# Six local attention layers on one Trainium2 core: scores ahead of the output product, softmax shift ahead of the residual addition

## The reference

```
for i in range(DEPTH):                       # DEPTH = 6
    x = attn_layer(shift_tokens(x), ...) + x
    x = ffn_layer(shift_tokens(x), ...) + x

q, k, v = split(x @ Wqkv); q = rope(l2norm(q)); k = rope(l2norm(k))
attn = softmax(mask(q k^T * 8))              # each window sees itself and the one before
out  = (attn v) @ Wo

xn = layernorm(x); a, gate = split(xn @ W1 + b1)
ffn = (a * gelu(gate)) @ W2 + b2
```

## Time and profile before

| | us |
|---|---|
| median of 3 runs | 3092.83 (3081.48 to 3099.36) |
| the profiled execution, its own time | 3103.04 |
| its span | 3101.3 |
| PE busy | 2707.9 (87%) |
| POOL busy | 1833.4 (59%) |
| DVE busy | 1738.0 (56%) |
| ACT busy | 1476.6 (48%) |

### The profile page before, as it was taken

The page is one execution under the profiler, slowest core; times in us unless marked ns, Lnnn a source line. Parts: engine busy times, 40 slices in busy tenths (PEclk is TensorE's granted clock), DMA queues, the critical chain, the costliest instruction groups (busy, mean ns, idle before and its releaser), DMA issues. The chain is left out here.

```text
span 3101.3 us, 91235 instructions
## 1 busy us (share of the span) xinstructions
PE 2707.9 (87%) x37375; PEld 1824.3 (59%) x37375; DVE 1738.0 (56%) x3395; ACT 1476.6 (48%) x2703; POOL 1833.4 (59%) x3112
## 2 busy tenths in 40 slices
PE   4859999965989999989999999999999958999977
PEld 1228888852666666666666666666666635455445
DVE  5832222214767776677767777777777635334324
ACT  3722232212656666566666566656665622233233
POOL 0045666405988888888888887888888711121111
PEclk9967898756999999999999999999999987577668
DMA  1001111102111212122212212121111100000000
GB/s 31 0 22 34 44 38 35 30 17 110 52 42 50 60 52 71 50 57 60 59 48 63 67 52 57 52 78 43 42 49 45 43 11 13 1 1 1 1 12 14
DMA packets 113143, 124.58 MB, mean 40 GB/s; under 512 B 40782, under 2 KB 71262, under 8 KB 111966
## 3 DMA queue, kind: packets, MB, share of 16 engines
q1 hardware_dynamic: 111808, 117.52, 13.8%
q10 hardware_dynamic: 926, 1.27, 0.1%
HBM read 35.89 MB, written 8.91 MB: 14 GB/s over the span
## 5 line engine op out<-in xcount | busy, mean ns | idle before, releaser
L1719 POOL TENSOR_TENSOR l_rot_a<-l_rot_a,l_rot_b 128x512 f32<-128x512 f32 x384 | 483.9, 1275 | 109.8 <-DVE l_rot_b L1579 109.3
L1207 PE MATMUL l_A<-l_wts,l_H 128*128 128x512 f32 x768 | 416.1, 626 | 25.5 <-ACT l_H L1520 21.5
L1573 DVE TENSOR_TENSOR l_rot_a<-l_A,l_tab 128x512 f32<-128x512 f32 x384 | 264.9, 690 | 288.5 <-ACT l_sq L1439 276.2
L1728 POOL TENSOR_TENSOR l_qk<-l_rot_a,l_rn 128x512 f32<-128x512 f32 x384 | 388.7, 1044 | 21.2 <-POOLq L1766 20.9
L1439 ACT ACTIVATE l_sq<-l_A 128x512 f32<-128x512 f32 x384 | 231.0, 601 | 131.9 <-PE l_A L1207 128.3
L1445 ACT ACTIVATE l_pT<-l_T 128x512 f32<-128x512 f32 x192 | 108.8, 595 | 374.0 <-PE l_T L1253 373.7
L1579 DVE TENSOR_TENSOR l_rot_b<-l_A,l_tab 128x512 f32<-128x512 f32 x384 | 261.4, 681 | 0.0
L1583 DVE TENSOR_REDUCE l_ss<-l_sq 128x8 f32<-128x512 f32 x384 | 259.5, 676 | 0.0
L2048 ACT ACTIVATE a_pT<-a_t 128x384 f32<-128x384 f32 (+1 forms) x256 | 111.1, 463 | 261.4 <-PE a_t L1946 261.3
L1308 PE MATMUL l_T<-ident,l_qk 128*128 128x128 f32 x1536 | 210.3, 279 | 19.6 <-POOL l_qk L1728 14.4
L1308 PEld LDWEIGHTS l_T<-ident,l_qk 128*128 128x128 f32 x1536 | 174.9, 142 | 84.1 <-issue 58.0
(11 more groups left out here) (340 smaller groups left out, 5948.0 us busy)
## 6 DMA issues: line engine op xcount, KB each, us to landing
l_vw<-l_vn SPq DMA_DIRECT2D x384, 128.0 KB
l_vw<-l_vn SPq DMA_DIRECT2D x360, 64.0 KB
l_wts<-in_l_wts SPq DMA_DIRECT2D x18, 650.0 KB, 4.9
c_lower_out<-c_amt SPq DMA_DIRECT2D x16, 384.0 KB, 2.5
c_inv<-c_first_in SPq DMA_DIRECT2D x16, 384.0 KB, 3.4
l_tab<-in_l_tables SPq DMA_DIRECT2D x6, 1024.0 KB, 5.1
l_wts<-in_l_wts SPq DMA_DIRECT2D x6, 635.5 KB, 5.3
result<-x SPq DMA_DIRECT2D x4, 256.0 KB, 2.3
```

The lines of the kernel that those rows point to most:

```text
L1207: pe.matmul(A[j % 2][:], cols(m), w_of(m)[:, C_QKV + 512 * j:C_QKV + 512 * j + 512], start=True, stop=True).then_inc(pq_done, 1)
L1573: dve.tensor_tensor(rot_a[p][:, j, :].rearrange("p (a d) -> p a d", d=DH), src.rearrange("p (a d) -> p a d", d=DH), table[:, a, t:t + 1, : ...
L1719: pool.tensor_tensor(rot_a[m % 2][:, j, :], rot_a[m % 2][:, j, :], rot_b[:, j, :], ALU.add).then_inc(rot_rdy, 1)
L1728: pool.tensor_tensor(qk[:, j, :].rearrange("p (a d) -> p a d", d=DH), rot_a[p][:, j, :].rearrange("p (a d) -> p a d", d=DH), rn[p][:, 8 * ...
```

## The change

In PE's loop `scores(n)` is moved ahead of `output(n-2)`. In DVE's loop `soft_shift(n)` is moved ahead of `add_back(n-2)`. No instruction, wait or buffer is added or taken away; ACT, POOL and the transfers keep their order.

```
@@ -1384,10 +1384,10 @@
                     masks(n)
                 if group_at(n, 4) is not None:
                     narrow(group_at(n, 4))
+                if has(n):
+                    scores(n, range(HP))
                 if has(n - 2):
                     output(n - 2)
-                if has(n):
-                    scores(n, range(HP))
                 if group_at(n, 2) is not None:
                     turn_norm(n, group_at(n, 2))
                 if has(n - 1):
@@ -1693,10 +1693,10 @@
                     rope(n + 2, 1)
                 if group_at(n, 4) is not None:
                     feed_back(group_at(n, 4))
+                if has(n):
+                    soft_shift(n)
                 if has(n - 2):
                     add_back(n - 2)
-                if has(n):
-                    soft_shift(n)
                 if has(n + 2):
                     rope(n + 2, 2)
                 if has(n):
```

## The result

| | us |
|---|---|
| before, median of 4 runs | 3096.1 (3081.48 to 3102.11) |
| with the change, median of 4 runs | 3251.2 (3242.33 to 3260.2) |
| ratio | 1.0508, 95% interval 1.0458 to 1.0559 |
| profiled execution, its own time | 3242.33 (before 3103.04) |
| its span | 3240.3 |

The forecast was 3286, with a range of 3235 to 3345. The direction and the range hold; the size, 193 us forecast for a median of 3093, was 155.

A forecast was written before the change was run, and what follows sets the result against it. PE was taken to bound the local layers. Slot costs of 7.25 us a period times 23.5 gave 170 us, plus 23 for the clock: 193 on 3103 gives 3296, less 10 against the median, 3286 us; range 3235 to 3345.

The forecast's parts named there:

- What bounds the kernel: Local layers: PE has 0.3, 0.0 and 0.5 us to spare in kinds 0, 1 and 2; 3.6 in kind 3.
- The scores' move brings nothing by itself: PE's loop: reordering scores and output gains nothing; the wait on ACT's copies it could relieve is 0.7 us in all.
- Kind 0: Slots like 48: the first half of the probabilities' transposes waits for DVE's shift and addition, costing 1.6 us.
- Kind 1: Slots like 49: DVE is held by `feed_back`, then shifts and adds before those transposes, costing 1.35 us.
- Kind 2: Slots like 50: PE already waits for the addition, so the whole shift ahead of it costs 2.5 us.
- The clock term: Slots of kind 2: lower clock after the longer wait in three of four, 1.3 us each, 23 us in all.
- Kind 3: Slots like 51: the shift adds 2.5 us, the wait at `turn_norm` absorbs 0.7, so the cost is 1.8 us.
- rival (a): POOL does not slip in kind 2, so `turn_norm` absorbs its delay and kind 3 costs nothing more: 3222 us; chance 0.06.
- The number of periods: Local layers: 94 slots have both tile n and tile n-2, taken as 23.5 four-tile periods paying the cost.
- Rival (b): The clock falls after every new wait, in kinds 0 and 1 too: up to 3446 us; chance 0.08.
- (c): Faster: an earlier softmax shift shortens the wait at `turn_norm`; half of its 50.5 us gives 3068 us; chance 0.03.
- (d): No measurable change: other PE waits hide the new one, though those in kinds 0 to 2 total 16.1 us; chance 0.03.

The follow-up runs named there:

- the two single-kind runs: The change made only in slots of kind 2, or only of kind 3, on the kernel before: 3137.0 us (+1.3%) and 3150.5 us (+2.1%).

## Why the prediction was right, and what was mis-sized

**What bounds the kernel: right.** PE has no slack in kinds 0 and 1, and a wait put there is paid in full: half 0 comes 1.45 and 1.15 us later in them, and the slots grow by 1.59 and 1.12. (POOL had 3.5 us to spare in slot 48, not the 1 to 3 of the prediction; nothing rests on it.)

**The scores' move brings nothing by itself: right**, shown by the run with PE's move alone, +0.6% and no gain.

**Kind 0, 1.6 forecast: 1.59, to the hundredth by luck.** Half 0 starts at 5.66 us, forecast 5.8, so 1.45 later than before. Most slots of kind 0 went from 16.58 to 18.07, 1.49 more; the rest of the mean comes from a few slots of 18.7 with an issue wait in them.

**Kind 1, 1.35 forecast: 1.12.** The sample misled me. Slot 49 belongs to a group whose `feed_back` has three instructions, one of them for the edge column; in every second group it has two and frees DVE about 0.25 us sooner. In the changed kernel half 0 starts 8.05 us into slot 49 and 7.79 into slot 53. The term was read from the dearer of the two.

**Kind 2, 2.5 and 0.75 x 1.3 for the clock, 3.5 in all: 2.85.** Half 0 comes 2.38 later on average (7.29 against 4.91 us into the slot), near the 2.5. The clock term came out near its size by a different way. The granted clock does fall in slots of kind 2, in 17 of the 22 from slot 4 to 91 (three in four was taken; before, in none); these 17 take 18.53 us and the other five 17.40, so it costs 1.1 a time, 0.87 a period where 0.98 was forecast. But the stretches are 3.4 us long, half the stretch of kind 3 on which I had priced them, and the 1.3 was meant as the share that POOL passes on. What the forecast left out in this kind is that some comes back behind half 0: in the five slots with the clock up PE goes from half 0 to the next masks in 10.10 us against 10.52 before, most of it idle time that is gone (0.22 instead of 0.56). The forecast had such hidden waits only at the lower end of its range. A stretch at the lower level, in slot 46:

```profile
1664.20:1667.60 3.40, 3.22 (x132) 2.41 (x132) 2.27 (x4) 1.98 (x4) 2.65 (x3) 0.51 0.02 5
```

**Kind 3, 1.8 forecast: 1.98.** In slot 50 POOL's `probs` slipped by 1.74 where 1.8 was worked out, and `turn_norm` waits 1.70 in slot 51 where 1.9 was. On average over slots 5 to 88 `turn_norm` starts 0.72 sooner in its slot (0.7 worked out), but its wait falls further, from 2.33 to 1.24, since PE comes to it later; that is why the sum is 27.3 where about 35 was forecast. Half 0 comes 1.67 later, and 0.3 more is lost behind it, where the lower clock now holds for 6.2 us of the slot instead of 5.5 (taken as no change). This step, on which rival (a) hung, is the one that the two single-kind runs test directly.

**The number of periods was the other mis-sized term.** Per period the change costs 7.5 us (80.8 - 73.3), not 8.2. And I multiplied by 23.5. From the masks of slot 4 to those of slot 92, 22 periods, the profiled executions differ by 162.0 us (1776.3 and 1614.3); the first four slots take 61.6 us in both, so the additions of slots 2 and 3 cost nothing there, and the last three slots add 3.9. What hides the first ones was not tried. That gives 166 us for the stretch. The rest of the program, which the change doesn't touch, took 27 us less in this execution (11.3 ahead of slot 0, 15.6 behind slot 95), which is how 139 comes out between the two profiled executions. That is chance: over the ten profiled kernels here the time ahead of slot 0 goes from 736.5 to 763.1 us and that behind slot 95 from 602.3 to 617.9, and no edit touches them. It also means that the 166 of the stretch and the 155 between the medians can't be told apart. The 27 us between the 193 forecast and these 166 are 0.7 a period too much, 16 us, nearly all of it from kind 2, and 11 us for counting 23.5 periods where some 22 have the cost.

**Rival (b), the clock after every new wait, did not come, and its mechanism is real.** In the changed kernel from slot 4 on no stretch at the lower level begins in kinds 0 or 1, where the waits are 0.7 to 1.2 us, as slot 54 had suggested. In the kernel with DVE's move alone the waits there are 2.5 us, and 34 such stretches begin in the 44 slots of kinds 0 and 1. The rule of the Trainium skill ("TensorE: Matmul & The Clock Gate", section "A second HAM failure mode: psum-queue depth-cycling"), that brief idling between groups of matmuls swings the clock, agrees with that kernel (20.60 us for slot 48 with the clock down, 19.30 for slot 44 with it up) and with kind 2 of the change, where waits of 2.3 to 3.0 us were followed by a fall in 17 of 22 slots. It does not agree with kinds 0 and 1 of the change, whose shorter waits leave PE at 2.4 GHz (PEclk 1.00 in slots 48 and 49). In these runs it takes more than that there is a wait: in kinds 0 and 1 no fall followed those of up to 1.2 us, and one followed those of 2.5 us in most slots, not in all.

**Rivals (c) and (d)**: POOL's wait for the reciprocal in kind 2 grew from nothing to 0.73 in slot 50, so an earlier shift shortened nothing; and the issue waits that the new wait could hide fell only from 16.1 to 11.6 us. The waits of half 0 for the addition sum to 201.9 us where some 230 was forecast: 1.2, 0.9, 2.7 and 4.2 by kind for 1.5, 1.2, 3.0 and 4.2.

## What to carry to other kernels

When two steps of a software pipeline share a buffer, the step that frees it belongs in its engine's queue at the moment when its input is ready, not behind work that is long and whose own consumer is not waiting; here 2.5 us of softmax ahead of a 0.6 us addition, with the product that it adds moved back as well, cost 7.5 us per four tiles, and moving the addition the other way won 2.1. Before starting a chain sooner, follow it to the step that ends it: the exponentials stood behind a square that stood behind the very transposes that the move delayed. And where slots alternate, take a term from every variant of the slot, and count how many periods really have it.

## What the runs showed of the hardware that I had not expected

A wait of PE can cost more than it lasts. The waits of 0.7 to 1.2 us in kinds 0 and 1 of the change cost about themselves. With DVE's move alone all slots of kind 0 have the same wait of 2.49 us; where the clock stayed up a slot mostly took 19.30 us, and where it fell to the lower level behind the wait, in 13 of 22, about 20.6. What decides between the two was not found. Lower stretches in the local layers are mostly 3.4 or 6.8 us long, some 10.2 and one, with the change in kind 3 alone, 13.7; one of 3.4 cost 1.1 us in kind 2 of the change and 1.3 in kind 0 with DVE's move alone. So the price of one can't be read from another place in the kernel.
